# Gathers written out on GpSimd, with row numbers read straight from the sorted tile

## The reference, cut to what matters

```python
# layer 1 (h = relu(layernorm(x)))
neigh = segment_sum(h[src], dst, 3125)
x = x + relu(relu(((1 + eps) * h + neigh) @ W1 + b1) @ W2 + b2)
# layer 2 (h = relu(layernorm(x)))
weights = einsum('rb,bio->rio', coefficients, bases)       # 16 x 128 x 128
out = h @ w_self.T
msg = sum over r of where(edge_type == r, h[dst] @ weights[r], 0)
x = x + out.at[src].add(msg)
```

## Time and profile before

| what | us |
|---|---|
| median of 3 runs | 1696.48 |
| span of the profiled execution (first to last instruction) | 1680.4 |
| what lies around the span, against the median | 16.1 |
| POOL busy | 911.3 (54%), of it the gathers 855.4 |
| PE busy | 933.3 (56%) |
| DVE busy | 749.9 (45%) |
| ACT busy | 413.4 (25%) |
| software DMA queue (the gathers) | 67.88 MB, 16.3% of 16 engines |
| hardware DMA queue | 33.09 MB, 7.2%, 40166 packets |

### The profile page before, as it was taken

How to read it: one execution, slowest core, us unless ns; L and a number is a source line. 1 busy time by engine, 2 the same in 40 slices (tenths; PEclk the granted TensorE clock), 3 DMA queues, 4 the chain that set the end, 5 groups by cost and what they waited for, 6 DMA issues and landing times.

```text
span 1680.4 us, 22781 instructions
## 1 busy us (share of the span) xinstructions
PE 933.3 (56%) x5317; PEld 656.0 (39%) x5318; DVE 749.9 (45%) x2213; ACT 413.4 (25%) x977; POOL 911.3 (54%) x843
## 2 busy tenths in 40 slices
PE   1355275666238676766678997145354345453535
PEld 0223153444114344443356444134353344343535
DVE  8888463665934444593457543012121122121213
ACT  4662263552014333443345431000000000000000
POOL 4354655555866566765560003746656656566562
PEclk9955586777657777876789998567676567665667
DMA  3010222224122222212221685211111111111113
GB/s 73 0 57 20 73 52 61 54 55 57 47 67 60 54 56 59 59 41 60 57 57 10 196 285 152 54 35 43 44 40 45 45 36 47 40 43 44 39 46 55
DMA packets 73343, 101.58 MB, mean 60 GB/s; under 512 B 43955, under 2 KB 52836, under 8 KB 73036
## 3 DMA queue, kind: packets, MB, share of 16 engines
q0 software_dynamic: 33120, 67.88, 16.3%
q1 hardware_dynamic: 40166, 33.09, 7.2%
HBM read 70.88 MB, written 29.60 MB: 60 GB/s over the span
## 4 chain that ended last, share of the span: by engine, by line
PE 44%; issue 28%; DVE 12%; another core or an unknown queue 12%; ACT 1%; DVEq 1%; DMA 1%; POOL 1%; ACTq 0%; SPq 0%; POOLq 0%
PE ps L802 16%; PE ps L819 15%; PE ps L824 9%; PE ps L893 4%; DVE spare L554 1%; DVE chunk_hot L616 1%; ACT place_val_b L443 1%; DVE spare L587 1%; DVE node_hot L668 1%; DVE chunk_f L590 1%; DVE place_val_a L619 1%; DVE w_rel L679 1%; DVE spare L678 1%; POOL gathered L411 1%
## 5 line engine op out<-in xcount | busy, mean ns | idle before, releaser
L411 POOL DMA_INDIRECT gathered<-h_table,row_stage x420 | 469.9, 1119 | 309.8 <-issue 247.4
L411 POOL DMA_INDIRECT gathered<-z_table,row_stage x405 | 385.5, 952 | 385.8 <-issue 229.0
L819 PE MATMUL ps<-gathered,node_hot 128*125 128x128 f32 x1620 | 289.6, 326 | 350.1 <-issue 328.5
L443 ACT ACTIVATE place_val_b<-place_hot,code_b 125x128 f16<-125x128 f16 x800 | 343.8, 522 | 523.1 <-DVE place_hot L612 361.2
L819 PEld LDWEIGHTS ps<-gathered,node_hot 128*125 128x125 f32 x1620 | 258.4, 235 | 381.4 <-issue 381.1
L668 DVE TENSOR_SCALAR node_hot<-iota_f,key_of 128x250 f32<-128x250 f32 x405 | 130.6, 364 | 512.5 <-remote 368.6
L802 PE MATMUL ps<-chunk_hot,place_val_a 125*128 125x405 f16 (+2 forms) x800 | 280.0, 364 | 117.1 <-DVE place_val_a L619 58.6
L802 PE MATMUL ps<-chunk_hot,place_val_b 125*128 125x387 f16 (+3 forms) x1200 | 274.5, 292 | 50.0 <-issue 41.2
L824 PE MATMUL ps<-node_hot,gathered 128*128 128x250 bf16 x1260 | 193.6, 299 | 156.8 <-issue 117.6
L616 DVE TENSOR_SCALAR chunk_hot<-iota_h,chunk_f 125x405 f16<-125x405 f16 (+2 forms) x800 | 210.2, 341 | 13.1 <-issue 12.6
L824 PEld LDWEIGHTS ps<-node_hot,gathered 128*128 128x128 bf16 x1260 | 127.6, 106 | 211.1 <-issue 188.0
(11 more groups left out here) (128 smaller groups left out, 319.1 us busy)
## 6 DMA issues: line engine op xcount, KB each, us to landing
z_table<-spare SPq DMA_DIRECT2D x50, 448.0 KB
gathered<-h_table,row_stage POOLq DMA_INDIRECT x420
gathered<-z_table,row_stage POOLq DMA_INDIRECT x405
z_table<-spare SPq DMA_DIRECT2D x50, 52.0 KB
h_table<-gathered SPq DMA_DIRECT2D x1, 2100.0 KB
x_sb<-in_x SPq DMA_DIRECT2D x1, 1400.0 KB
out<-x_sb SPq DMA_DIRECT2D x6, 224.0 KB
row_stage<-row_of SPq DMA_DIRECT2D x81, 2.5 KB
```

The costliest lines, as they stand in the source:

```text
L411: pool.indirect_dma_start(place.rearrange("p j d -> p (j d)") if s < 2 else place, None, table, bass.IndirectOffsetOnAxis(ap=row_stage[s][ ...
L443: nc.scalar.activation(place_val_b[:, buf, i, :], place_hot[:, buf, :, i], ACT.Copy, scale=code_b[l][:, bass.ds(batch * BATCH + (c0 + i), ...
L819: last = T.matmul(psf[0:NP, bass.ds(offs[i] + half * D, D)], node_hot_of[s][:, k % HOTS[s], half * NP:(half + 1) * NP], gathered_of[s][:, ...
```

## The change

The loops of POOL are written out: 825 gathers stand one behind another. Each reads its column of `row_of[s]`. In front of a group POOL itself waits for `nhot_used` with the count that SP waited for before, and in front of a sort once for `decoded` and for the stored table. `stage_rows`, `row_stage`, `staged` and `begun` go, and with them 199 small DMAs and their waits from SP.

```diff
-        row_stage = [sb(f"row_stage{s}", [P, GROUPS[s], GROUP[s]], I32) for s in range(3)]
...
-        def stage_rows(sp, s):
-            sp.wait_ge(decoded, s + 1)
...
-                    sp.wait_ge(nhot_used, r * RING[s] + (CHUNKS_BEFORE[s] + (g + 1) * GROUP[s] + RING[0] - RING[s]))
-                    sp.dma_start(row_stage[s][:, g, :],
-                                 row_of[s][:, bass.ds(r * RING[s] + g * GROUP[s], GROUP[s])]).then_inc(staged[s][g], 16)
...
-                with nc.gpsimd.Fori(0, ROUNDS[s]) as r:
-                    for g in range(GROUPS[s]):
-                        if s < 2:
-                            pool.wait_ge(h_stored, 32)
-                        else:
-                            pool.wait_ge(z_stored[-1], 32 * (2 * TILES // Z_BUFS))
-                        pool.wait_ge(staged[s][g], r * 16 + 16)
-                        pool.sem_inc(begun, 1)
-                        for i in range(GROUP[s]):
-                            place = gathered_of[s][:, g * GROUP[s] + i]
...
-                                bass.IndirectOffsetOnAxis(ap=row_stage[s][:, g, i:i + 1], axis=0)).then_inc(got[s][g], 16)
+                pool.wait_ge(decoded, s + 1)
+                for k in range(CHUNKS[s]):
+                    slot = k % RING[s]
+                    if k % GROUP[s] == 0:
+                        if k >= RING[s]:
+                            pool.wait_ge(nhot_used, RING[0] + CHUNKS_BEFORE[s] + k + GROUP[s] - RING[s])
+                        elif s and k < RING[s - 1]:
+                            pool.wait_ge(nhot_used, RING[0] + CHUNKS_BEFORE[s] - RING[s - 1] + min(k + GROUP[s], RING[s - 1]))
+                    place = gathered_of[s][:, slot]
+                    pool.indirect_dma_start(
+                        place.rearrange("p j d -> p (j d)") if s < 2 else place, None, table,
+                        bass.IndirectOffsetOnAxis(ap=row_of[s][:, k:k + 1], axis=0)).then_inc(got[s][slot // GROUP[s]], 16)
```

More of the change, by code:

```diff
@@ L219, in build @@
         decoded, keys_decoded = sem("decoded"), sem("keys_decoded")
-        staged = [[sem(f"staged{l}_{g}") for g in range(GROUPS[l])] for l in range(3)]
-        begun = sem("begun")
         got = [[sem(f"got{l}_{g}") for g in range(GROUPS[l])] for l in range(3)]
@@ L302, in build @@
         block = ctx.enter_context(nc.Block())
-        def stage_rows(sp, s):
-            sp.wait_ge(decoded, s + 1)
-            if s:
-                for g in range(GROUPS[s]):
-                    sp.wait_ge(nhot_used, CHUNKS_BEFORE[s] - RING[s - 1] + min((g + 1) * GROUP[s], RING[s - 1]) + RING[0])
-                    sp.dma_start(row_stage[s][:, g, :],
-                                 row_of[s][:, g * GROUP[s]:(g + 1) * GROUP[s]]).then_inc(staged[s][g], 16)
-            with nc.sync.Fori(min(s, 1), ROUNDS[s]) as r:
-                for g in range(GROUPS[s]):
-                    sp.wait_ge(nhot_used, r * RING[s] + (CHUNKS_BEFORE[s] + (g + 1) * GROUP[s] + RING[0] - RING[s]))
-                    sp.dma_start(row_stage[s][:, g, :],
-                                 row_of[s][:, bass.ds(r * RING[s] + g * GROUP[s], GROUP[s])]).then_inc(staged[s][g], 16)
         @block.sync
@@ L338, in _ @@
                 sp.dma_start(h_rows[p0:p1, :, :, :], h_parts[p0:p1, :, :, :]).then_inc(h_stored, 16)
-            stage_rows(sp, 0)
-            stage_rows(sp, 1)
             for t in range(TILES):
@@ L351, in _ @@
                                      z_stage[p0:p1, slot, :]).then_inc(z_stored[slot], 16)
-            stage_rows(sp, 2)
             for g in range(NBANK):
@@ L394, in _ @@
                 table = h_table if s < 2 else z_table
-                if s == 2:
-                    for q in range(Z_BUFS - 1):
+                if s < 2:
+                    pool.wait_ge(h_stored, 32)
+                else:
+                    for q in range(Z_BUFS):
                         pool.wait_ge(z_stored[q], 32 * (-(-(2 * TILES - q) // Z_BUFS)))
-                with nc.gpsimd.Fori(0, ROUNDS[s]) as r:
-                    for g in range(GROUPS[s]):
-                        if s < 2:
-                            pool.wait_ge(h_stored, 32)
-                        else:
-                            pool.wait_ge(z_stored[-1], 32 * (2 * TILES // Z_BUFS))
-                        pool.wait_ge(staged[s][g], r * 16 + 16)
-                        pool.sem_inc(begun, 1)
-                        for i in range(GROUP[s]):
-                            place = gathered_of[s][:, g * GROUP[s] + i]
-                            pool.indirect_dma_start(
-                                place.rearrange("p j d -> p (j d)") if s < 2 else place, None, table,
-                                bass.IndirectOffsetOnAxis(ap=row_stage[s][:, g, i:i + 1], axis=0)).then_inc(got[s][g], 16)
+                pool.wait_ge(decoded, s + 1)
[10 more added lines that the diff above has]
+                        bass.IndirectOffsetOnAxis(ap=row_of[s][:, k:k + 1], axis=0)).then_inc(got[s][slot // GROUP[s]], 16)
         @block.scalar
```

## The result

The changed kernel took 1590.47 us (median of 4 runs, 1590.24 to 1593.8) against 1694.97 us for the kernel before, timed beside it (4 runs, 1687.71 to 1698.53): 0.9391 of it, 95% interval [0.9367, 0.9415]. The profiled execution has a span of 1588.4 us, 92.0 less than that of before (1680.4). The other 12 us are no part of the two traces: the changed kernel's profiled execution is one of its timed runs (1590.24 us, 1.8 above its span), while that of before, with the same 1.8 added, comes to 1682.2 us, faster than any of its timed runs (1687.71 at the least).

A forecast was written before the change was run, and what follows sets the result against it. POOL was taken to pace the kernel, pausing on a full ring while PE, starved by gathers, caught up. Layer 2 -15, layer 1 -30, starts -3 gave -48, said 50: 1680.4 - 50 + 16.1 = 1646.5 us; range 1606 to 1698.

The forecast's parts named there:

- What bounds the kernel: Gather stretches: POOL is the pacemaker; gathers starve PE, the full ring stops POOL, PE catches up; 48 long pauses.
- The last 0.78: Handover of 2.67 us from PE to POOL: this part stays, so each pause gets only 1.75 us shorter.
- What is late next: PE's free window shrinks with the pause, so more pauses come: gain 15 us in layer 2, 30 in layer 1.
- Starts: Sorts 0, 1 and 2 each begin one landing earlier: 3 x 1.7 us at most, 3 counted.
- Code: Fetching 825 gathers in line: four or so more blocks, taken as 0; +24 us if uncovered.
- The small packets: SP's 199 copies leave the hardware queue: nothing counted, bounds 0 to -10 us.
- The 16.1 us around the span: Profiled span 1680.4 against the median 1696.5; the difference was added back in the forecast time.
- A: All gather stretches: nothing given back, each of 48 pauses 1.75 us shorter, 84 us gained, 1612 us; chance 0.15.
- C: PE's free window: short pauses cut bursts below break-even (13.8 chunks in layer 2), +26 us, 1722; chance 0.10.
- B: PE's free window sets throughput, so all is given back: 1680 to 1700 us, say 1690; chance 0.22.
- The signs named ahead: Layer 2: pauses of 4.4 us, 22 or so, cycles of 16 chunks, gather 0.9 us after PE, total near 95 us.
- The last sentence of the forecast: PE's creeping stretches: if they change in kind, for instance vanish with the staging copies, the time falls below 1606 us.

The follow-up runs named there:

- g2: Kernel before with gathers and SP's loop written out, staging copies still waited for, POOL held one group ahead of PE in layer 2: 2010.79 us (chip 6).
- i2: Changed kernel with POOL one group ahead in layer 2 and PE's count relayed by SP through a one-word copy in both layers: 2148.64 us (chip 15).
- f0: The changed kernel without an edit, timed again on chip 2: 1407.88 us, 0.9964 of the kernel before.
- i1: Changed kernel with POOL one group ahead in layer 2, SP also making the staging copies, for which nobody waits: 2004.9 us (chip 15).
- e4: Changed kernel with POOL waiting for the ring's place of every chunk instead of every group: 1404.89 us, 0.9984 of the kernel before (chip 9).

## Why the prediction was wrong

**What bounds the kernel: right.** POOL paced the stretches, its pauses were PE's creeping plus the handover, and the gain came out of the pauses. What the profile of one execution could not tell is that this holds on some chips only.

**"The last 0.78 is POOL's own way from a semaphore to the gather, and stays": wrong.** It goes with the loop. In the loop of before a copy lands at 1165.47, POOL adds to `begun`, and the gather starts at 1166.27, 0.80 later. Written out it starts 0.26 us after the landing: in g2, and in i2 too, in layer 1 beside a creeping PE as in layer 2 (medians, from the semaphore's updates in the traces). In the changed kernel it is 0.28 us from PE's free start at 1159.78 to the gather at 1160.06. Whether the loop's registers or the addition to `begun` took the 0.5 us was not tried. So 2.4 us leave the handover and not 1.75. In the rows of the table below with 6, 9 and 15 gathers a pause is shorter by just that, 2.3 to 2.4 us (means, worked out from the order in time on POOL; number of pauses in brackets); after 49 it is 4.8. Sort 1 scatters more (16 gathers: 5.19 us in 2 pauses, then 2.48 in 7).

| gathers in the burst | before | changed |
|---|---|---|
| 6 (sort 0) | 3.74 us (4) | 1.40 us (10) |
| 9 (sort 0) | 4.39 us (3) | 2.02 us (2) |
| 10 (layer 2) | none | 2.35 us (32) |
| 15 (layer 2) | 5.52 us (3) | 3.15 us (1) |
| 20 (layer 2) | 6.38 us (14) | none |
| 49 (layer 2) | 10.52 us (1) | 5.74 us (1) |

**"What is late next" is the step that failed.** The forecast let the pause lose the handover alone and kept "PE free some 3.8 us after the last gather as before". The table shows that the rest of a pause grows with the burst before it: take off the handover (2.67 before, 0.28 now), and after 15 gathers it is 2.85 and 2.87 us, after 10 it is 2.1, after 20 it is 3.7. (Two bursts of 5 in the changed kernel, with 2.67 us each, do not fit.) So more and shorter bursts, which the forecast booked as a loss, make each pause shorter once more: PE is free after 2.1 us now. Where the creeping lies within a burst fits this. PE's matmul records of layer 2 per us (four are a chunk), by the time since POOL restarted:

| us since the restart | 0 to 3 | 3 to 6 | 6 to 9 | 9 to 12 | 12 to 16 | 16 to 20 |
|---|---|---|---|---|---|---|
| before | 6.21 | 9.00 | 3.27 | 0.67 | 0.61 | 0.40 |
| changed | 4.35 | 5.44 | 1.71 | 0.78 | (ended) | |

For some 6 us after a restart PE is not held up (until 1173.03 before, 6.8 us after the restart; until 1165.60 now, 5.5 us after it); from 9 us on it does hardly anything. A burst of 19.4 gathers (24 us) has 15 us of that, one of 10 (12.3 us) has 3. In numbers of a cycle: the forecast had a free window of 7.7 us, 16.5 chunks and a pause of 4.35 beyond the 0.30, 1.51 us a chunk. It was a window of 5.8 us, 10 chunks and 2.07, 1.25 + 2.07 / 10 = 1.457, seen 1.465.

The price of a chunk in the window was off as well. The forecast's 0.61 us a chunk at the mean is 0.75 in the window at 1159.78 (31 records in 5.82 us): it is the fast end that goes. Two stretches of PE's free window before, then two now (columns as in the earlier trace rows, the third number from the end is the granted clock):

```profile
1166.30:1169.30 3.00, 3.00 (x21) 3.00 (x21) 1.81 (x6) 0.00 (x0) 2.39 (x3) 0.69 0.15 36
1169.30:1173.00 3.70, 3.70 (x35) 3.54 (x33) 0.54 (x2) 0.00 (x0) 2.79 (x4) 1.00 0.25 51
...
1160.00:1163.00 3.00, 3.00 (x15) 3.00 (x16) 1.82 (x6) 0.00 (x0) 2.33 (x3) 0.50 0.08 22
1163.00:1166.00 3.00, 2.73 (x19) 2.57 (x18) 0.39 (x2) 0.00 (x0) 2.39 (x3) 0.79 0.26 66
```

Before, PE begins its window at a clock of 0.50 and does the last 35 records of it at 1.00, in 3.70 us. Now most of it passes at the lower clock, and when the clock stands at 1.00 PE is held up again (4 records from 1166 to 1168 us). So the shorter window also has the slower chunks, and the shorter pauses have to outweigh that too. Layer 2 gained 39.5 us where 15 were booked, layer 1 61.2 where 30 were. A give-back exists, but elsewhere: 10.5 us in the two stretches where no gather runs, since POOL now ends farther ahead of PE (133 records against 96 behind the last gather).

**Starts: right as far as seen** (3 booked; 1.8 at the first sort, f0's 3.3 in all fits). **Code: right**, and by its own count: four more loads on q14 (which the forecast, with its "one instruction queue", had not read), none with a price that shows. **The small packets: right** at nothing, 1.4 us in i1. **The 16.1 us around the span: misread.** Only 1.8 us lie around a span here (the changed kernel's profiled run, and every experiment's, has its time and its span 1.8 to 1.9 us apart); the other 14 are a profiled execution of before that was faster than the median. The sum took the 50 us off the median all the same, so no harm came of it.

**The rivals.** A (nothing given back, 84 us) was nearest, and for its own reason wrong: the number of pauses did not stay, it nearly doubled. C foresaw the bursts of 10 and called them slower, with a break-even at 13.8 chunks; it kept the pause at 4.35. With bursts of 10 and only the measured 2.4 off the handover it would have been right, 1.25 + (6.1 - 2.4) / 10 = 1.62 us a chunk. The held-up part, 3.8 to 2.1 us, decided the sign. B is excluded by layer 1.

**The signs named ahead.** Pauses of 4.4 us in layer 2: 2.4. Some 22 of them: 37. Cycles of 16 chunks: 10. Gather 0.9 us after PE is free: 0.28. Long pauses of layer 2 near 95 us beyond the usual 0.30: 79.8 by the rule used here, against 118.7 before. The last sentence of the forecast, that a change in kind of the creeping would be faster than the range, is near what happened: it got shallower, but by shorter bursts, not by the missing copies.

**The Trainium skill's rule.** "SBUF — State Buffer", section "SBUF: two separate sides", says that DMA and compute engines do not slow each other. f0's trace agrees (320 of PE's records in 100 us beside 80 gathers); the first measurement's doesn't seem to (19 records in 22.0 us beside gathers, 62 in the next 9.5), though no run shows that PE is held up at SBUF.

What stays open: what the creeping of PE (and of DVE, which has the multiples of 0.71 us too) is, and why chip 15 has it and chips 2, 6, 9 and 10 don't. The runs show when it comes and goes (with gathers in flight, some 6 us after they start), not what it is. Whether POOL restarting chunk by chunk (e4) helps on a chip that creeps was not tried there.

## What to carry to other kernels

A pause in a producer and consumer cycle is rarely a constant: read it as handover plus what the consumer needs to get free, plot the second against the burst before it, and only then say what a shorter handover gives back. Take a DMA out of a handover (1.67 us here, while passing the count over another engine costs 0.04), but it pays only where the ring runs full; where the ring covers it, it is worth nothing at all. And before a change is judged by one chip, time the kernel before on several: the same change gave 6% in one measurement and 0.4% on another chip.

## What the runs showed of the hardware

- The same kernel took 1694.97 us in the first measurement and 1691.22 on chip 15, and 1409.44, 1411.21, 1409.89 and 1409.2 us on chips 9, 2, 6 and 10, each within 1%. What sets the slow ones apart in the traces is that PE's and DVE's instructions come at multiples of some 0.71 us while gathers of the software queue run.
- On such a chip a burst of gathers leaves PE its pace for some 6 us and then takes it; bursts of 5 with PE at work between them cost nothing (1010.7 against 1008.5 us for 405 chunks on the two kinds of chip).
- From PE's count to a waiting POOL's gather: 0.27 us directly, 0.31 over SP's semaphore, 1.76 over a copy of one word, 1.94 over a copy of 128 x 5.
- From the landing of a copy to a waiting POOL's gather: 0.8 us in the loop of before, 0.26 written out.
- 825 gathers in line take 44 loads on one instruction queue where the loops take 40, with 17 on the other alike, at the same pace (1.25 us).
